# A slot table for the expert rows, an even split of the first expert weights, and filler products on TensorE

## The chip, the cores and the metric

The kernel runs as one program on one core of a Trainium2 chip. Its time is the device time of one execution in microseconds (us). Everything is float32, except one product in bfloat16.

## What is computed

The reference is a small vision transformer with four layers over 16 images of 37 tokens (592 tokens) with 192 features. The arithmetic of the earlier sublayers is not touched by the change. The last sublayer is a mixture of eight experts, of which each token takes the two with the highest gates:

```python
logits = xf @ Wr + br                       # xf: 592 x 192, eight experts
gates = jax.nn.softmax(logits, axis=-1)
top_g, top_i = jax.lax.top_k(gates, 2)
out = jnp.zeros_like(xf)
for e in range(8):
    w_e = jnp.sum(top_g * (top_i == e), axis=-1)
    h = jax.nn.gelu(xf @ W1[e] + b1[e], approximate=False)   # W1[e]: 192 x 768
    y = h @ W2[e] + b2[e]                                     # W2[e]: 768 x 192
    out = out + w_e[:, None] * y
```

`xf` is the layer-normalised `h`, and the result is added to `h`.

## The kernel before

**Tower.** The 16 images are held as eight pairs; a pair fills 101 partitions (37 tokens, a gap up to 64, 37 tokens). Each layer is cut into phases (`T` transposes the normalised rows, `F` and `K` make keys and queries, `R` turns them, `S` scores, `W` values, `X` turns the probabilities, `O` the output of attention, `Z` turns it, `P` projects), and every phase is done for two halves of four pairs, q = 0 and q = 1. The string `ORDER` interleaves the phases of the two halves into `SCHEDULE`, and each of the five engines walks that list in its own stream, so an engine that waits holds back all that stands behind it in the list. A PSUM bank is a job: `start_job` on TensorE waits until the bank's last user has been read, `end_job` tells that it is filled. `A` to `G` are the sublayers before the last, `H` is the last one.

**Routing (`H`).** Phase `H,G` makes the gate logits of a half: for each pair three products whose contraction has 128, 64 and 1 rows. `route_gate` on VectorE marks the two picked experts (`picked`). Phase `H,C` (job `cum`) sums on TensorE how many tokens before this one picked the same expert, on top of the first row of that expert's region. `route_spots` on VectorE turns it into two row numbers for each token. GpSimd then scatters: for each of the 16 (pair, choice) it sends 101 rows of 194 numbers (the features, the gate and the token's own row number) to the DRAM tensor `expert_rows`, line L552, which had been filled with blank rows. While these run, TensorE counts the tokens of each expert and makes the bias part (`eb`), VectorE adds it to `h` and runs `plan_tiles`, which tells which expert the spare tiles belong to.

**Expert loop.** Each expert has one tile of 128 rows, and there are nine spare tiles, 17 in all. When all scatters have landed, SyncE loads the tiles from `expert_rows` (`load_x`, L407). For each tile TensorE turns the rows (`turn_x`, L1261 and L1262, into 128 and 64 feature rows), makes 12 products with W1 (`fc1`, L1274: six column blocks, for each one product over 128 rows and one over 64) and 6 products with W2 (`fc2`, L1285); ScalarE does the gelu (L730), VectorE copies the turned rows and weighs the result by the gate (`weigh_y`, L1175, three buffers `yb`), and GpSimd adds the 128 rows to `rows_out` in DRAM with an indirect DMA (L560). Each of these waits until the one before has landed (`added`), since two tiles may hold the same token. The order on TensorE is turn(j+1), fc1(j), fc2(j-1). There are three sets of weights. SyncE loads the next ones in one stream: W1 of tile j+3 when fc1(j) is done, then the rows of tile j+6 when add j has landed, then W2 of tile j+3 when fc2(j) is done. Last, SyncE copies `rows_out` to the output.

In the profile's names `arena_k` holds the tiles' rows, the weighed results and the third set of weights, `rep` the hidden rows after the gelu, `bank` a PSUM bank. A float32 product shows as two matmul records, a transpose as one.

## Time and profile before

| | |
|---|---|
| median of 3 runs (lowest, highest) | 630.85 us (627.7, 631.73) |
| the profiled execution's own time | 634.18 us |
| its span, first to last instruction | 632.4 us |
| TensorE busy | 512.4 us (81%) |
| VectorE, ScalarE, GpSimd busy | 269.5, 183.7, 120.2 us |
| mean granted TensorE clock | 0.829 of full speed |
| DMA | 39.29 MB, mean 62 GB/s |

### The profile page before, as it was taken

Reading aid. Unit: us, or ns where it says so; the run is one execution under the profiler, and the core shown is the slowest. Engines: PE = TensorE matmul, PEld = TensorE weight load, DVE = VectorE, ACT = ScalarE, POOL = GpSimd, SP = SyncE. Lnnn points to the kernel's source line nnn. Section 1 sums busy time; section 2 is a strip of 40 time slices with the busy share of each in tenths; the row PEclk is TensorE's granted clock in tenths of the full one; section 3 lists DMA queues with packets and bytes.
Section 4 is the critical chain, followed back from the end, with each engine's and each line's share of the span. In section 5 each row is a group of like instructions: output and inputs, shape, how many; then the busy total and the mean of one; then the engine's idle time right before and its main releaser. Section 6 shows DMA issues by size and latency. Waiting matters only on the chain.

```text
span 632.4 us, 8623 instructions
## 1 busy us (share of the span) xinstructions
PE 512.4 (81%) x3314; PEld 414.0 (65%) x3314; DVE 269.5 (43%) x735; ACT 183.7 (29%) x439; POOL 120.2 (19%) x127
## 2 busy tenths in 40 slices
PE   4899999796967798999999579755503999999992
PEld 4876766695846676877578458754402788777872
DVE  5467545435474745635355666853400011111100
ACT  0222323212323616346452255221100222222120
POOL 2220100011120110111001230117861021221121
PEclk9979569878886969999999879855555599999897
DMA  8800000000290000000050000200113137666742
GB/s 320 205 2 0 1 1 1 2 1 1 66 250 11 0 1 2 2 0 1 1 150 1 1 2 2 76 1 13 24 17 78 37 96 200 168 202 187 219 106 41
DMA packets 23725, 39.29 MB, mean 62 GB/s; under 512 B 6167, under 2 KB 16399, under 8 KB 23474
## 3 DMA queue, kind: packets, MB, share of 16 engines
q1 hardware_dynamic: 16484, 35.40, 19.3%
q0 software_dynamic: 7056, 2.69, 3.4%
q8 instruction: 27, 0.44, 0.3%
q10 hardware_dynamic: 144, 0.64, 0.3%
q14 instruction: 14, 0.11, 0.1%
HBM read 31.51 MB, written 7.91 MB: 62 GB/s over the span
## 4 chain that ended last, share of the span: by engine, by line
PE 64%; DVE 15%; POOL 6%; issue 5%; ACT 5%; DMA 3%; POOLq 0%; SPq 0%; DVEq 0%; ACTq 0%
PE bank L1274 14%; PE bank L1285 6%; PE bank L1231 5%; PE bank L1503 5%; PE bank L1251 5%; PE bank L1209 4%; POOL expert_rows L552 4%; PE bank L1411 4%; PE bank L1455 3%; PE bank L1298 3%; PE bank L1240 3%; PE bank L1470 2%; ACT xn L581 2%; DVE stats L758 2%; PE bank L1352 2%
## 5 line engine op out<-in xcount | busy, mean ns | idle before, releaser
L480 POOL TENSOR_TENSOR rstd<-rstd_tmp,minus_half 101x4 f32<-101x4 f32 x20 | 20.5, 1025 | 333.1 <-DVE rstd_tmp L768 333.1
L1274 PE MATMUL bank<-arena_k,weights 128*128 128x128 f32 (+1 forms) x288 | 68.5, 355 | 0.4 <-issue 0.2
L1274 PEld LDWEIGHTS bank<-arena_k,weights 128*128 128x128 f32 (+1 forms) x288 | 48.4, 210 | 19.9 <-issue 6.5
L1251 PE MATMUL bank<-weights,rep 96*111 96x192 f32 (+1 forms) x320 | 56.8, 327 | 0.0
L1175 DVE TENSOR_SCALAR arena_k<-bank,arena_k 128x192 f32<-128x192 f32 x17 | 7.1, 417 | 113.5 <-PE bank L1285 113.5
L1251 PEld LDWEIGHTS bank<-weights,rep 96*111 96x111 f32 (+1 forms) x320 | 52.2, 175 | 2.2 <-issue 2.1
L560 POOL DMA_INDIRECT rows_out<-arena_k x17 | 26.4, 1551 | 122.6 <-DVE arena_k L1175 112.9
L1231 PE MATMUL bank<-nT,weights 96*96 96x296 f32 (+1 forms) x144 | 42.9, 446 | 3.8 <-DVE nT L783 2.5
L730 ACT ACTIVATE rep<-bank,parameters 128x128 f32<-128x128 f32 x48 | 14.2, 366 | 87.2 <-PE bank L1274 87.2
L552 POOL DMA_INDIRECT expert_rows<-x_rows,spot_row x16 | 35.6, 2223 | 11.5 <-issue 10.6
L1503 PE MATMUL bank<-weights,oT 96*101 96x192 f32 (+1 forms) x144 | 34.9, 412 | 3.0 <-issue 1.8
L581 ACT ACTIVATE xn<-h,minus_mean_rstd,rstd 101x192 f32<-101x192 f32 x56 | 25.9, 535 | 37.5 <-POOL minus_mean_rstd L487 37.4
L1442 PE MATMUL bank<-vblk,et 111*37 111x51 f32 (+1 forms) x640 | 25.1, 243 | 13.9 <-ACT et L692 7.1
L1231 PEld LDWEIGHTS bank<-nT,weights 96*96 96x96 f32 (+1 forms) x144 | 24.9, 178 | 17.5 <-issue 7.5
L1209 PE MATMUL bank<-constants,x_y 101*96 101x101 f32 x144 | 21.6, 321 | 17.6 <-DVE x_y L1070 10.3
L1442 PEld LDWEIGHTS bank<-vblk,et 111*37 111x37 f32 (+1 forms) x640 | 24.0, 143 | 17.1 <-issue 16.2
L1503 PEld LDWEIGHTS bank<-weights,oT 96*101 96x101 f32 (+1 forms) x144 | 30.7, 220 | 6.6 <-ACT oT L645 4.4
L1411 PE MATMUL bank<-arena_k,qT 96*64 96x222 f32 (+1 forms) x320 | 34.3, 368 | 0.8 <-DVE arena_k L796 0.8
L805 DVE TENSOR_TENSOR vblk<-bank,constants 111x384 f32<-111x384 f32 x40 | 21.6, 554 | 23.8 <-PE bank L1251 15.7
L1261 PE MATMUL bank<-constants,arena_k 128*128 128x128 f32 x17 | 5.3, 313 | 32.5 <-DMA arena_k<-expert_rows 32.5
L1209 PEld LDWEIGHTS bank<-constants,x_y 101*96 101x96 f32 x144 | 18.8, 167 | 19.6 <-issue 12.9
L730 ACT ACTIVATE rep<-bank,expert_b 128x128 f32<-128x128 f32 x54 | 15.9, 365 | 51.1 <-PE bank L1274 51.1
(243 smaller groups left out, 891.9 us busy)
## 6 DMA issues: line engine op xcount, KB each, us to landing
weights<-in_w SPq DMA_DIRECT2D x12, 576.0 KB, 4.4
weights<-in_w SPq DMA_DIRECT2D x12, 384.0 KB, 4.5
expert_rows<-blank_row SPq DMA_DIRECT2D x1, 3977.0 KB, 22.3
arena_k<-in_w SPq DMA_DIRECT2D x5, 576.0 KB, 4.2
arena_k<-in_patches SPq DMA_DIRECT2D x4, 606.0 KB, 8.4
weights<-in_w SPq DMA_DIRECT2D x12, 192.0 KB, 5.3
arena_k<-in_w SPq DMA_DIRECT2D x5, 384.0 KB, 4.4
arena_k<-expert_rows SPq DMA_DIRECT2D x17, 97.0 KB, 2.1
```

The source lines that it names most:

```text
L552: g.indirect_dma_start(slots, bass.IndirectOffsetOnAxis(spot_row[0:ROWS, r, k:k + 1], 0), xa[0:ROWS, r, k, :], None, bounds_check=XROWS - ...
L560: g.indirect_dma_start(rows_out, bass.IndirectOffsetOnAxis(xt[j % XBUFS].bitcast(I32)[:, XW - 1:XW], 0), yb[j % 3], None, bounds_check=T + ...
L581: ins = sc.activation(dst, src, ACT.Identity, scale=rstd[0:ROWS, r:r + 1], bias=nmr[0:ROWS, r:r + 1])
L730: sc.activation(hT[b][:, m], PS[2 * b + half][:, TILE * x:TILE * x + TILE], ACT.Gelu, bias=bias[:, m:m + 1]).then_inc(gelu_done, 1)
L1209: last = nc.tensor.transpose(ps[0:96, 128 * p:128 * p + ROWS], src[0:ROWS, p, 96 * s:96 * s + 96], ident[0:ROWS, 0:ROWS])
L1231: last = mm(o, w(seg, k, col + 96 * s, 96), nt(k, q), start=(k == 0), stop=(k == 1 and not lora))
L1251: last = mm(o, nrep[q][k][0:96 + k, im], w(n + "_qkv", k, 2 * D, D), start=(k == 0), stop=(k == 1 and n != "B"))
L1274: last = mm(PS[2 * (j % 2) + half][:, TILE * x:TILE * x + TILE], w1b[j % WSETS][0:r, k, 128 * m:128 * m + 128], xT[j % 2][0:r, k], start=( ...
L1285: last = mm(PS[4 + j % 2][:, 0:D], hT[j % 2][:, m], w2b[j % WSETS][:, m], start=(m == 0), stop=(m == MT - 1))
L1411: last = mm(ps[GAP * i:GAP * i + m, HH * TOK * s:HH * TOK * s + HH * TOK], qT[s][:, TOK * im:TOK * im + m], kblk[q][s][:, im % Q8].rearran ...
L1442: last = mm(ps[GAP * pr:GAP * pr + m, VW * i + gw * g:VW * i + gw * (g + 1)], et[q][:, g, TOK * (im - Q8 * q):TOK * (im - Q8 * q) + m], vb ...
L1503: last = mm(ps[0:ROWS, D * i:D * i + D], pair_cols(oT, k, 2 * c + i), wp, start=(k == 0), stop=(k == 1))
```

## The change

**Slot table.** The scatters, the blank fill of `expert_rows` and the copy of the rows on GpSimd are gone. ScalarE writes the normalised rows of `H` to `xn` as in other layers, and SyncE stores them to `rows_x` in DRAM (8 direct DMAs) as soon as they are there. For each token and choice, VectorE compares the spot with the 42 first spots of the 41 columns (eight experts by five tiles deep, and one empty), which gives the column and the place in it (`hit`, 101 x 1024 a half); GpSimd multiplies the column mark with the token number and with the gate (`entry`, three operations a half); and TensorE sums 16 products of `hit` and `entry` into a table of 128 places by 41 columns, with token, gate and an occupied mark (job `table`). `slot_tables` turns it into `slot_row` and `slot_gate`. A tile's rows are then gathered by GpSimd with one indirect DMA (`gather`), six ahead of the loop and one behind each add from then on. For the nine spare tiles GpSimd reads the column from `tile_of` and copies two columns each. `plan_tiles` now runs ahead of the `eb` additions on VectorE.

**Weights.** The first expert weights and the turned rows are split into 96 and 96 rows, not 128 and 64. W1 is loaded by three DMAs, not two. VectorE copies the turned rows in one operation, not two. SyncE's stream in the loop has no wait on `added` any more.

**Fillers.** `keep_busy` runs n products of the 128 x 128 identity with itself into the bank that the next job will use, ahead of that job's waits. There are 198 of them by a fixed table.

```diff
+IDLE_T = {("B", 1): 11, ("D", 1): 8, ("F", 1): 25, ("G", 1): 9, ("H", 0): 10, ("H", 1): 12}
+IDLE_R = 19
+IDLE_O = {("B", 0): 12, ("C", 0): 12, ("C", 1): 15, ("G", 1): 14}
+IDLE_CUM, IDLE_SLOT, IDLE_ROWS = 9, 6, 8
...
             def load_w1(e, b):
-                sp.dma_start(w1b[b][:, 0], w1[e][:, 0]).then_inc(w1_loaded[b], 16)
-                sp.dma_start(w1b[b][0:D - 128, 1], w1[e][0:D - 128, 1]).then_inc(w1_loaded[b], 16)
+                sp.dma_start(w1b[b][:, 0], w1[e][0:HALF, 0]).then_inc(w1_loaded[b], 16)
+                sp.dma_start(w1b[b][0:128 - HALF, 1], w1[e][HALF:128, 0]).then_inc(w1_loaded[b], 16)
+                sp.dma_start(w1b[b][128 - HALF:HALF, 1], w1[e][0:D - 128, 1]).then_inc(w1_loaded[b], 16)
...
-            sp.wait_ge(scattered, 16 * TOPK * PAIRS)
-            for j in range(XBUFS):
-                load_x(slice(j * REGION, j * REGION + TILE), j)
+            for q in octs:
+                sp.wait_ge(*xn_ready.at(("H", q)))
+                store_rows(rows_x, xn, q, x_stored)
...
-                    sp.wait_ge(added, 16 * j + 16)
-                    load_x(slice(row, row + TILE) if n < NE else bass.ds(row, TILE), n % XBUFS)
...
                 if (n, ph) == ("H", "C"):
+                    pool.wait_ge(*begins_ready.at(q))
+                    link(g.tensor_tensor(col[:, :, 2], past_begin[0:ROWS, :, 0:COLS], past_begin[0:ROWS, :, 1:], ALU.subtract))
+                    link(g.tensor_tensor(col[:, :, 0].rearrange("p (c k) x -> p c k x", k=TOPK), col[:, :, 2].rearrange("p (c k) x -> p c k x", k=TOPK), which, ALU.mult))
                     pool.wait_ge(*spots_ready.at(q))
-                    for r in range(P8 * q, P8 * q + P8):
-                        for k in range(TOPK):
-                            g.indirect_dma_start(slots, bass.IndirectOffsetOnAxis(spot_row[0:ROWS, r, k:k + 1], 0), xa[0:ROWS, r, k, :], None,
-                                                 bounds_check=XROWS - 1, oob_is_err=False).then_inc(scattered, 16)
+                    g.tensor_tensor(col[:, :, 1], col[:, :, 2], gate, ALU.mult).then_inc(*entries_ready.inc(q))
...
+            def gather(j):
+                at = slot_row[:, DEEP * j:DEEP * j + 1] if j < NE else tile_row[:, j - NE:j - NE + 1]
+                g.indirect_dma_start(xt[j % XBUFS], None, rows_x, bass.IndirectOffsetOnAxis(at, 0),
+                                     bounds_check=T + TILE - 1).then_inc(x_loaded[j % XBUFS], 16)
+            pool.wait_ge(slots_ready, 1)
+            pool.wait_ge(x_stored, 16 * 4 * len(octs))
+            for j in range(XBUFS):
+                gather(j)
+            pool.wait_ge(plan_ready, 2)
+            for j in range(SPARE):
+                col = pool.value_load(tile_of[0:1, 1, j:j + 1], min_val=0, max_val=COLS - 1)
+                g.tensor_copy(tile_row[:, j:j + 1], slot_row[:, bass.ds(col, 1)]).then_inc(spares_ready, 1)
+                g.tensor_copy(tile_gate[:, j:j + 1], slot_gate[:, bass.ds(col, 1)]).then_inc(spares_ready, 1)
             for j in range(TILES):
                 pool.wait_ge(y_ready, j + 1)
                 if j:
                     pool.wait_ge(added, 16 * j)
...
+                if j + XBUFS < TILES:
+                    pool.wait_ge(xT_filled, j + 1)
+                    gather(j + XBUFS)
...
+            slot_tables()
+            plan_tiles()
             for c in range(PAIRS // 2):
                 add_bank(("eb", c), h[0:ROWS, 2 * c:2 * c + 2], h[0:ROWS, 2 * c:2 * c + 2])
-            plan_tiles()
...
+            def keep_busy(j, n):
+                b, k = where[j]
+                if k:
+                    pe.wait_ge(bank_read[b], k)
+                for _ in range(n):
+                    mm(PS[b][:, 0:128], ident, ident, start=True, stop=True)
...
-                        for k, r in enumerate((128, D - 128)):
-                            last = mm(PS[2 * (j % 2) + half][:, TILE * x:TILE * x + TILE], w1b[j % WSETS][0:r, k, 128 * m:128 * m + 128], xT[j % 2][0:r, k],
+                        for k in range(2):
+                            last = mm(PS[2 * (j % 2) + half][:, TILE * x:TILE * x + TILE], w1b[j % WSETS][:, k, 128 * m:128 * m + 128], xT[j % 2][:, k],
                                       start=(k == 0), stop=(k == 1))
```

On TensorE, from the gate logits of the second half to the first products of the expert loop, the instructions stood like this before (`picked,every` is the running sum, `disp` the turned gates, `expert_b` the bias part):

```order
574 L1352 MATMUL bank<-parameters,ones 101x8
575 L1359 MATMUL bank<-picked,before 101x32
576 L1362 MATMUL bank<-picked,every 101x32 x4
...
580 L1363 MATMUL bank<-region_base,ones 101x32
581 L1508 MATMUL bank<-picked,every 1x8 x8
582 L1514 MATMUL bank<-constants,disp 8x101 x8
583 L1522 MATMUL bank<-expert_b,x_y 101x192 x8
584 L1261 MATMUL bank<-constants,arena_k 128x128
585 L1262 MATMUL bank<-constants,arena_k 64x128
```

and now, with the fillers as L1272 and L1613 and the table as L1445:

```order
587 L1424 MATMUL bank<-parameters,ones 101x8
588 L1272 MATMUL bank<-constants 128x128 x9
589 L1432 MATMUL bank<-picked,before 101x32
590 L1435 MATMUL bank<-picked,every 101x32 x4
...
594 L1436 MATMUL bank<-region_base,ones 101x32
595 L1272 MATMUL bank<-constants 128x128 x6
596 L1445 MATMUL bank<-vblk,arena_e 128x123 x16
597 L1594 MATMUL bank<-picked,every 1x8 x8
598 L1600 MATMUL bank<-constants,disp 8x101 x8
599 L1608 MATMUL bank<-expert_b,x_y 101x192 x8
600 L1613 MATMUL bank<-constants 128x128 x8
601 L1331 MATMUL bank<-constants,arena_k 96x128 x4
```

Fillers came in at three places, the table's 16 products between the running sum and the count, and the turned rows have 96 partitions both times.

On GpSimd, from the second half's routing to the end, before:

```order
94 L552 DMA expert_rows<-x_rows,spot_row 5248x194 x8
95 L545 COPY x_rows<-x_rows 101x4x192
96 L552 DMA expert_rows<-x_rows,spot_row 5248x194 x8
97 L560 DMA rows_out<-arena_k 720x192 x17
```

and now (the rows of the eight further spare tiles are left out):

```order
99 L568 TENSOR_TENSOR vblk<-vblk,share 101x8x41 [waits spots_ready,pool_chain]
100 L573 DMA arena_k<-rows_x,slot_row 128x192 [waits blanked,x_stored,slots_ready,entries_ready]
101 L573 DMA arena_k<-rows_x,slot_row 128x192 x5
102 L584 TENSOR_LOAD tile_of [waits plan_ready]
...
105 L585 COPY tile_row<-slot_row 128x1
106 L586 REGISTER_ALU
107 L586 COPY tile_gate<-slot_gate 128x1
...
156 L594 DMA rows_out<-arena_k,slot_row 720x192 [waits y_ready,rows_stored,spares_ready]
157 L573 DMA arena_k<-rows_x,slot_row 128x192 [waits xT_filled]
158 L594 DMA rows_out<-arena_k,slot_row 720x192 [waits added,y_ready]
159 L573 DMA arena_k<-rows_x,slot_row 128x192 [waits xT_filled]
```

The 16 scatters are gone, six gathers and 18 small copies stand ahead of the first add, and a gather stands between every two adds up to the eleventh.

## Rows read from the trace of the kernel before

**Rows 1.** The page, part 2: granted TensorE clock in 40 slices of the span

```profile
PEclk9979569878886969999999879855555599999897
```

**Rows 2.** The chain of waits from 433 us: start, length, what

```profile
433.64 4.86 PE bank L1352 x23
...
475.21 7.21 DMA expert_rows<-x_rows,spot_row
482.44 2.01 DMA arena_k<-expert_rows
...
485.81 8.75 PE bank L1274 x24
...
515.56 4.80 PE bank L1274 x24
520.36 2.15 PE bank L1285 x12
```

**Rows 3.** Busy time by stretches: PE, PEld, DVE, ACT, POOL, clock, DMA share, GB/s

```profile
61.50:88.80 27.30, 25.16 (x106) 19.93 (x103) 14.20 (x44) 6.84 (x15) 1.71 (x3) 0.50 0.00 1
...
406.20:484.60 78.40, 29.95 (x197) 26.73 (x197) 26.63 (x109) 9.74 (x22) 40.87 (x24) 0.50 0.10 16
484.60:508.60 24.00, 23.87 (x71) 17.45 (x71) 2.25 (x9) 3.54 (x12) 0.00 (x0) 0.50 0.24 59
508.60:580.30 71.70, 71.70 (x378) 56.64 (x378) 7.42 (x29) 18.27 (x65) 15.56 (x10) 1.00 0.62 175
```

**Rows 4.** The same, sum of five stretches at the lower clock between 122.9 and 372.1 us

```profile
sum 61.50, PE 44.90 PEld 38.59 DVE 26.95 ACT 17.43 POOL 7.73; mean PE 8.98 PEld 7.72 DVE 5.39 ACT 3.49 POOL 1.55
```

**Rows 5.** TensorE in order of time: last bracket the idle time before and its end

```profile
76.81 1.58 PE L1209 MATMUL bank<-constants,xn 101*96 101x101 f32 x8 [0.58 <-ACT xn L581]
121.93 2.81 PE L1442 MATMUL bank<-vblk,et 111*64 111x51 f32 x64 [2.96 <-ACT et L692]
155.60 4.25 PE L1209 MATMUL bank<-constants,x_y 101*96 101x101 f32 x24 [5.01 <-DVE x_y L1070]
271.62 6.24 PE L1455 MATMUL bank<-nT,weights 96*128 96x296 f32 x24
362.39 1.58 PE L1209 MATMUL bank<-constants,xn 101*96 101x101 f32 x8 [6.32 <-ACT xn L581]
431.43 0.94 PE L1217 MATMUL bank<-constants,x_rows 101*128 101x101 f32 x4 [6.04 <-ACT x_rows L581]
```

**Rows 6.** GpSimd's groups of instructions: count, busy us, mean ns, idle before

```profile
L552 POOL DMA_INDIRECT expert_rows<-x_rows,spot_row x16 | 35.6, 2223 | 11.5 <-issue 10.6 <-POOL x_rows L545 0.9
L500 POOL TENSOR_TENSOR h<-h,parameters 101x768 f32<-101x768 f32 x4 | 7.5, 1866 | 8.3 <-ACT xn L581 8.2
```

**Rows 7.** The adds (L560) to landing: from 508 to 540 us, then 544 to 600

```profile
DMA to landing us min/median/max: 3.5/3.6/4.0
...
DMA to landing us min/median/max: 5.2/6.0/7.7
```

**Rows 8.** GpSimd in order of time: the fifth last add and the last

```profile
600.61 1.54 POOL L560 DMA_INDIRECT rows_out<-arena_k  x1 [6.95 <-DMA rows_out<-arena_k]
...
624.86 1.54 POOL L560 DMA_INDIRECT rows_out<-arena_k  x1 [2.74 <-DMA rows_out<-arena_k]
```

**Rows 9.** VectorE in order of time, second half's routing, last bias addition, plan

```profile
438.92 0.19 DVE L886 TENSOR_REDUCE gate_rows<-bank 101x4 f32<-101x32 f32 x1 [5.38 <-PE bank L1352]
439.37 0.42 DVE L891 TENSOR_TENSOR et<-gates 101x256 f32<-101x256 f32 x1
441.20 0.19 DVE L897 SCALAR_TENSOR_TENSOR picked<-gates,valid 101x32 f32<-101x32 f32 x1
...
452.15 0.56 DVE L850 TENSOR_TENSOR h<-bank,h 101x384 f32<-101x384 f32 x1 [0.72 <-PE bank L1522]
452.63 0.14 DVE L940 COPY plan<-bank 1x8 f32<-1x8 f32 x1
...
455.50 0.15 DVE L955 TENSOR_SCALAR tile_of<-plan 1x9 int32<-1x9 f32 x1
```

More of the change, by code:

```diff
@@ L121, in phase_jobs @@
     if (n, ph) == ("H", "C"):
-        return [("cum", q)]
+        return [("cum", q)] + [("table",)] * q
     if ph == "G":
@@ L921, in route_spots @@
[L921 to L925 removed]
+                mark(v.tensor_reduce(high, at, AX.X, ALU.max))
+                link(v.tensor_reduce(both, at, AX.X, ALU.add))
@@ new lines, in route_spots, with slot_tables @@
+                link(v.scalar_tensor_tensor(depth[0:ROWS], depth[0:ROWS], -float(TILE), spots, ALU.mult, ALU.add))
+                v.tensor_tensor(hit[0:ROWS, n * q:n * q + n], depth[0:ROWS].unsqueeze(2).broadcast_to([ROWS, n, TILE]),
+                                lane[0:ROWS].unsqueeze(1).broadcast_to([ROWS, n, TILE]), ALU.is_equal).then_inc(*hits_ready.inc(q))
+                dve.wait_ge(*hits_ready.at(q))
+            def slot_tables():
+                j = ("table",)
+                dve.wait_ge(*filled(j))
+                row, gate, busy = (bank(j)[:, COLS * x:COLS * x + COLS] for x in range(3))
+                link(v.tensor_scalar(unused[:], busy, 1.0, spare_row[:], ALU.subtract, ALU.mult))
+                v.tensor_tensor(slot_row[:], row, unused[:], ALU.add).then_inc(slots_ready, 1)
+                v.tensor_copy(slot_gate[:], gate).then_inc(*freed(j))
+                dve.wait_ge(*evacuated(j))
@@ L1363, in _ @@
                     end_job(("cum", q), mm(ps[0:ROWS, 0:w8_], ones[:, 0:ROWS], base[:], start=False, stop=True))
+                    if q:
+                        keep_busy(("table",), IDLE_SLOT)
+                        ps = start_job(("table",))
+                        n_ = PAIRS * TOPK
+                        for x in range(n_):
+                            if x % (n_ // 2) == 0:
+                                pe.wait_ge(*hits_ready.at(x // (n_ // 2)))
+                                pe.wait_ge(*entries_ready.at(x // (n_ // 2)))
+                            last = mm(ps[:, 0:3 * COLS], hit[0:ROWS, x], entry[0:ROWS, x].rearrange("p w c -> p (w c)"), start=(x == 0), stop=(x == n_ - 1))
+                        end_job(("table",), last)
                 elif ph == "G":
@@ L1525, in _ @@
             wait_evacuated(*[max((j for j in order if where[j][0] == b), key=lambda j: where[j][1]) for b in range(8)])
+            for _ in range(IDLE_ROWS):
+                mm(PS[6][:, 0:128], ident, ident, start=True, stop=True)
             turn_x(0)
```

169 lines of the change are left out of this document (99 added, 70 removed).

## The prediction

> **What bounds the kernel now.** I read the clock row of the page first, then the chain of waits, then stretches. The clock row shows that TensorE is granted full speed in the middle but half of it in patches on the left and for a long piece on the right [rows 1]. The chain shows two things about the last quarter. From 438 to 484.6 us it lies not on TensorE but on the scatters: 16 of them at 2.2 us with 0.3 us between, 7.21 us until the last has landed, 2.01 us for loading the first tile [rows 2, 6]. TensorE is busy 30 of 78 us there [rows 3]. Then the expert loop is TensorE alone: from 508.6 to 580.3 us it is busy without a break [rows 3], and one tile costs 4.80 (fc1) + 2.15 (fc2) + 0.22 (two transposes) = 7.17 us [rows 2]. Its first fc1 took 8.75 us, since the clock stood at 0.50 until 508.6 us [rows 2, 3]. So the last part has two limits in a row, GpSimd's scatters and TensorE's products; the part before 406 us is TensorE with short waits for VectorE and ScalarE, after which the clock falls [rows 5].
>
> **Part 1, the even split.** Before, 24 matmul records of 128 moving columns take 4.80 us, 0.200 us each, and the six products of fc2, though with 192 columns, only 2.15/12 = 0.179 us each [rows 2]. Fewer columns should not take longer. The nearest record with 96 rows on both sides and 128 stationary columns is L1455: 24 records of 296 columns in 6.24 us, 0.260 each [rows 5], by columns 0.112 us for 128. I take it, since it has the same rows, the same stationary width and the same clock: fc1 = 24 x 0.112 = 2.7 us. The ends: 2.7 us, and 4.80 us if rows don't matter. What stands out is that fc1 changes between 128 and 64 rows after every product, and L1455 does not. The Trainium skill ("TensorEngine Tiling (Array Packing)", Key Properties) says that a change of the tiling mode drains the engine, and that contractions of up to 64 rows are tiled; by it the split pays, as the row of L1455 has it. Another page of the Trainium skill ("TensorE: Matmul & The Clock Gate", LDWEIGHTS) says that loading weights takes a time by columns and not by rows; by that alone fc1 stays as it is (second rival). A tile on TensorE then costs 2.7 + 2.1 + 0.2 = 5.0 us. ScalarE (six gelus) and VectorE are at 18 and 7 of 72 us in the loop [rows 3] and stay hidden. The third W1 DMA costs nothing as long as weights are ahead.
>
> **Part 2, routing.** Counted on the clock of before, from the transposes of the second half at 431.4 us [rows 5]. If the fillers hold the full clock: transposes 0.9 (four records take 0.94 cold [rows 5], eight as much at full clock), an estimate of 0.6 for the copies, gate logits 3.0 (4.86 cold [rows 2]; half is 2.4), the pick on VectorE 2.4 as before [rows 9], the running sum's 22 records at some 0.1 each 2.1, together 440.4. New on VectorE: seven small operations of 0.1 to 0.2 us, two of 336 elements at 0.5, and the hit marks of 1024 elements: 256 take 0.42 [rows 9], so at most 1.7. Sum 4.3, 444.7. GpSimd's three operations of 328 elements run beside it: 768 take 1.87 [rows 6], so 0.8 each, hidden. The table: the first half's eight products are done while VectorE works, the second half's are 16 records, 1.8 us; VectorE makes the columns in 0.5: 447.0. From here two branches. The gather: issue 0.8, landing 3.6 (an add of 128 rows when DMA is quiet [rows 7]), 451.4. No gather is in the trace; the ends are 2.0 (a direct load of a tile [rows 2]) and 7.2 (a scatter [rows 2]), which is 449.8 and 455.0. I take the add because it has the same queue and 128 rows. The other branch is VectorE's: the plan now comes first, 3.0 us (452.63 to 455.65), then four bias additions of 0.56 [rows 9], and only after them TensorE may run its last 8 fillers, 1.8 us: 454.1. So what sets the start of the loop is this branch, and I take 454.5 against 484.6 before: 30 us earlier. The late filler is in that sum; without it 1.8 us less.
>
> **Part 3, GpSimd in the loop.** This is where I expect the next limit. An add waits until the last one has landed. One began at 600.61 less 6.95 idle less 1.55, at 592.1; with 7.7 us to landing that is 599.8, and the next began at 600.6 [rows 7, 8]. So the period of adds is landing + 0.8. The gather between (about 1.6 us of GpSimd) hides inside the flight. The landing is 3.5 to 4.0 us early in the loop and 5.2 to 7.7, median 6.0, from 544 to 600 us [rows 7], when SyncE's weight loads run right beside the adds. That gives 4.4 to 6.8 us a tile, against TensorE's 5.0. Before, 7.17 hid either. The same 1.2 MB of weights now come every 5 to 6 us, staggered by fc1 and fc2, so that some load is nearly always in flight, but rarely both: I take 5.8 (the middle, 5.6, leaning to the loaded rows) for 13 tiles and 5.0 for the last three, whose loads are over; 16 periods make 90.4 us. The first add: two transposes and copy 0.8, two fc1 5.4, one fc2 2.1, weighing and issue 1.2, that is 9.5 after the start: 464.0. The six gathers (six times 1.9 from 447.8) and the 18 small copies are done by about 461, so they cost nothing; if the copies took over 0.35 us each more than I think, they would delay it. From the start of the last add to the end of the span it was 632.4 - 624.86 = 7.5 us [rows 8]. End: 464.0 + 90.4 + 7.5 = 561.9 us.
>
> **Part 4, the fillers ahead of the last sublayer.** A filler product is two records of 128 columns, 0.22 us at full and 0.45 at half clock. Where it stands in a wait that is long enough it is free: 12 take 2.7 in a wait of 2.96, 19 take 4.3 in 5.01, 25 take 5.6 in 6.32 [rows 5]; the other sites up to 407 us, four more with waits of 2.9 to 5.3, are alike. After five of these stretches TensorE worked 44.9 us at half clock [rows 4]; at full clock it would be 22.4. Much of that is behind other engines too, VectorE being busy 27.0 of 61.5 us [rows 4], so I count 60%: 13.5. The last O, gate logits and transposes before the second half's give 3.5 more. The site of half 1 in B has no wait to speak of, 0.58 us [rows 5], and 11 products cost 4.9 us cold, in a stretch of 25.2 busy us at half clock [rows 3]; if they bring the full clock forward by some us, it evens out, and I set it at nothing, with -4 to +4. Sum: 17 us, from 8 (a third of the cold work) to 25 (all of it).
>
> **Sum.** Span 561.9 - 17 = 544.9 us; with the 1.8 us around it 546.7, against 634.2 of the profiled execution. That one lay 3.3 above the median, so the forecast for the median is 543.4 us. Low end: GpSimd never late, 16 x 5.0, and 25 from the fillers: 464.0 + 80 + 7.5 - 25 - 1.5 = 525. High end: 13 x 6.8 + 15, and 8 from the fillers: 464.0 + 103.4 + 7.5 - 8 - 1.5 = 565.4.
>
> **Rivals.** *TensorE stays the bound.* Adds land in 4.2 us or less throughout, as they did until 540 us [rows 7]; the period is 5.0: 464.0 + 80 + 7.5 - 17 - 1.5 = 533 us. For it: weights no longer come in one burst with the add. Against: more bytes a microsecond. Chance 0.22.
>
> *The split brings nothing.* fc1 stays at 4.80, as it would if a product's time went by columns alone (the weight rule above). Against it speaks L1455. Period 7.2, first add at 468.2: 468.2 + 115.2 + 7.5 - 17 - 1.5 = 572.4 us. Chance 0.10.
>
> *The fillers don't hold the clock.* Then they run at 0.45 us and overrun seven of the waits by 2 to 5 us each, 23 in all, with 4 for the site in B and 2 in the last sublayer, nothing is given back, and routing runs cold, 8 us more: 561.9 + 29 + 8 - 1.5 = 597.4 us. For it: 24 us of unbroken work from 484.6 did not lift the clock [rows 3]. Against: those were fc1's products with their change of rows, and 128-row products leave no holes. Chance 0.09.
>
> *Slower than before.* Gathers and adds share GpSimd's queue. If an add could not run beside a gather, and a gather landed as late as a scatter did (median about 6.8, last 7.2 [rows 2]), each of the first 11 periods would be 6.0 + 6.8 + two issues of 0.8 = 14.4, the other five 6.8: 464.0 + 192.4 + 7.5 - 17 - 1.5 = 645 us. It decides from 13.1 us a period on. Nothing in the trace shows such a series; scatters there started every 2.5 us while the earlier ones were in flight. Chance 0.02.
>
> **Chances.** My forecast 0.56, the rivals as given, 0.01 for the rest. The range 524 to 573 takes in the bounds, the first and the second rival, and leaves out about 0.12. About 1% is what three runs with this spread (627.7 to 631.7) can tell from no change. Faster by over 1%: 0.97; within 1%: 0.01; slower: 0.02.
>
> **What the profile after would show.** Part 1: fc1 at 2.6 to 2.8 us a tile. Part 2: the loop starting at about 437.5 (454.5 - 17), 47 us earlier in all, with the last bias addition and the fillers just ahead of it. Part 3: GpSimd's adds idle before on "DMA rows_out", not on VectorE, starts 5 to 6.5 us apart, and TensorE with holes of up to 1.5 us a tile. Part 4: clock digits of 9 to the left of the loop. The forecast is wrong if the landing under load is not near 5, if GpSimd's dynamic copies are slow enough to delay the first add past 464, or if holes in the loop bring the clock down again.

## The result, and the profile after

The changed kernel takes **568.09 us** (median of four runs, 562.93 to 570.62) against 629.28 for the kernel before beside it (four runs, 625.57 to 631.73): ratio 0.902, 95% interval 0.894 to 0.910. From here on medians are of all runs of a kernel, while ratios with their intervals leave out its slower runs, so that the two need not agree. The forecast was 543.4 us with a range of 524 to 573: faster as said, inside the range, 25 us above the number. The profiled execution took 562.93 us with a span of 561.2; it is the fastest of its four, 5.2 below their median.

The marks below stand for both profiled executions, in us from the start of the span. "First transposes" are those of the gate's second half; "first turn" is the first transpose of gathered rows, where the expert loop begins.

| | before | after | forecast for after |
|---|---|---|---|
| first transposes | 431.4 | 419.6 | 414.4 (431.4 - 17) |
| first turn | 484.6 | 449.65 | 437.5 |
| first add | 509.0 | 460.1 | 447.0 |
| last add | 624.9 | 553.4 | 537.4 |
| end of the span | 632.4 | 561.2 | 544.9 |
| fc1 of one tile at full clock, from its start to that of fc2 | 4.80 | 2.68 | 2.7 |
| mean period of the adds | 7.24 | 5.83 | 5.65 |

The page, part 2, in the 40 slices of the span (compare [rows 1]):

```profile
POOL 3040100002111010102200012310220544434332
PEclk9999777989989899999999999799976899998895
```

The patches of half clock on the left have become 7s and 8s, and the long cold piece before the loop is down to a 7 and a 6 (slices 30 and 31); the middle is as it was. The stretches that answer to [rows 3], with the same columns: the last sublayer and the routing, the first tile, and two parts of the loop:

```profile
398.20:449.60 51.40, 41.12 (x294) 38.65 (x291) 30.78 (x111) 8.96 (x19) 14.34 (x18) 0.78 0.11 28
449.60:461.20 11.60, 11.52 (x92) 11.02 (x91) 2.01 (x5) 4.42 (x15) 3.52 (x20) 0.94 0.36 100
461.20:508.60 47.40, 45.30 (x345) 44.72 (x344) 6.79 (x18) 16.40 (x58) 20.09 (x16) 0.97 0.98 273
```

The DMA share in the loop is 0.98 where it was 0.62, since the same weights now come in less time. TensorE is no longer busy without a break there. TensorE in order of time from the first transposes into the loop (compare [rows 2, 5]; L1272 and L1613 are fillers):

```profile
419.63 0.96 PE L1286 MATMUL bank<-constants,xn 101*128 101x101 f32 x8 [2.47 <-ACT xn L616]
421.80 0.91 PE L1424 MATMUL bank<-parameters,nT 128*101 128x8 f32 x4 [1.21 <-issue]
...
426.98 3.99 PE L1272 MATMUL bank<-constants 128*128 128x128 f32 x18
...
433.97 1.95 PE L1445 MATMUL bank<-vblk,arena_e 101*128 101x123 f32 x16
438.06 2.05 PE L1445 MATMUL bank<-vblk,arena_e 101*128 101x123 f32 x16 [2.14 <-DVE arena_e L969]
...
441.66 2.91 PE L1608 MATMUL bank<-expert_b,x_y 8*101 8x192 f32 x16 [0.29 <-issue]
446.10 3.76 PE L1613 MATMUL bank<-constants 128*128 128x128 f32 x16 [1.53 <-DVE h L885]
449.65 1.06 PE L1331 MATMUL bank<-constants,arena_k 128*96 128x128 f32 x4
...
453.92 2.84 PE L1344 MATMUL bank<-arena_k,weights 96*128 96x128 f32 x24
456.60 2.12 PE L1355 MATMUL bank<-weights,rep 128*128 128x192 f32 x12
```

With two halves of 96 rows fc1 is 24 records in 2.84 us here, and fc2 starts 2.68 us after it: in order of time the last record counts to its end, which overlaps the next one. The like figures of before are 4.97 and the 4.80 of [rows 2]; its TensorE in order of time has

```profile
536.90 4.97 PE L1274 MATMUL bank<-arena_k,weights 128*128 128x128 f32 x24
```

The fillers are 0.118 us a record where the clock is up (experiment 12 below, 42 in 4.96 us), and 0.22 to 0.235 in the two groups here: both stand where the clock is down, and the second is what TensorE does right before the loop. VectorE in the same place (compare [rows 9]):

```profile
436.78 1.22 DVE L969 TENSOR_TENSOR arena_e<-depth,lane 101x1024 f32<-101x1024 f32 x1
...
440.60 0.20 DVE L979 TENSOR_TENSOR slot_row<-bank,unused 128x41 int32<-128x41 f32 x1
...
440.95 0.15 DVE L996 COPY plan<-bank 1x8 f32<-1x8 f32 x1
...
443.86 1.93 DVE L885 TENSOR_TENSOR h<-bank,h 101x384 f32<-101x384 f32 x4
```

The hit marks, the table's rows, then the plan (2.9 us), then the four bias additions, then the fillers: the order that the forecast walked through, later by what the next section takes apart. GpSimd in order of time, gathers (L573), one of the small copies, adds (L594), and then the adds' time to landing before and after 540 us (compare [rows 6 to 8]):

```profile
441.79 1.34 POOL L573 DMA_INDIRECT arena_k<-rows_x,slot_row  x1 [5.07 <-DVE slot_row L979]
...
452.50 0.18 POOL L586 COPY tile_gate<-slot_gate 128x1 f32 x1
460.12 1.64 POOL L594 DMA_INDIRECT rows_out<-arena_k,slot_row  x1 [7.43 <-DVE arena_k L1236]
...
489.40 1.58 POOL L594 DMA_INDIRECT rows_out<-arena_k,slot_row  x1 [4.35 <-DMA rows_out<-arena_k,slot_row]
491.29 1.06 POOL L573 DMA_INDIRECT arena_k<-rows_x,tile_row  x1 [0.32 <-issue]
496.84 1.58 POOL L594 DMA_INDIRECT rows_out<-arena_k,slot_row  x1 [4.49 <-DMA rows_out<-arena_k,slot_row]
```

```profile
DMA to landing us min/median/max: 3.6/5.5/6.6
...
DMA to landing us min/median/max: 3.4/3.5/3.5
```

The copies are over 7.4 us before the first add. From then on an add waits for the landing of the last one, 7.4 us from one to the next here, and only after it may the gather go. The waits between 461 and 540 us:

```profile
POOL rows_out L594 <- DMA rows_out<-arena_k,slot_row: 23.2, 7, 4.5
...
POOL rows_out L594 <- DMA rows_out<-arena_k,tile_row: 11.9, 3, 5.8
...
PE bank L1331 <- DMA arena_k<-rows_x,tile_row: 5.7, 3, 2.1
```

Ten adds waited 35.1 us for the one before. TensorE waited three times, 5.7 us, and not for the adds but for gathers that stand behind them in the queue. From these waits alone either could be what sets the loop's pace. The chain of waits that ends the span says more; its shares from 460 to 554 us:

```profile
by line: DMA rows_out<-arena_k,slot_row 46.0%; DMA rows_out<-arena_k,tile_row 38.8%; issue 12.9%; POOLq L182 1.9%; POOLq L594 0.5%; DVE arena_k L1236 0.5%; POOLq L573 0.3%; POOLq L592 0.3%; DVEq L1232 0.0%
```

84.8% of it is adds in flight, and TensorE's last product ended at 542.8 us, 10.6 us before the last add began. Experiment 7 tests it.

### The profile page after: what moved, and what is told of

Its sections match the earlier page's. It is cut to its first block, busy times and chain, and to the rows that moved or that the text cites. A ratio compares the mean times of both kernels' runs of the same rounds, so it can differ in the third digit from the quotient of the medians.

```text
span 561.2 us, 9551 instructions
## 1 busy us (share of the span) xinstructions
PE 490.3 (87%) x3742; PEld 421.8 (75%) x3742; DVE 274.5 (49%) x725; ACT 183.6 (33%) x439; POOL 108.3 (19%) x150
## 4 chain that ended last, share of the span: by engine, by line
PE 50%; DVE 19%; DMA 15%; issue 6%; ACT 6%; POOL 2%; POOLq 1%; SPq 0%; DVEq 0%; ACTq 0%
DMA rows_out<-arena_k,slot_row 8%; PE bank L1320 7%; DMA rows_out<-arena_k,tile_row 6%; PE bank L1300 6%; PE bank L1589 5%; PE bank L1495 5%; PE bank L1368 3%; PE bank L1541 3%; PE bank L1278 3%; PE bank L1309 3%; PE bank L1556 3%; ACT xn L616 3%; DVE stats L793 2%; PE bank L1424 2%; DVE arena_e L848 1%
## 5 line engine op out<-in xcount | busy, mean ns | idle before, releaser
L497 POOL TENSOR_TENSOR rstd<-rstd_tmp,minus_half 101x4 f32<-101x4 f32 x20 | 20.5, 1024 | 321.1 <-DVE rstd_tmp L803 321.1
L1272 PE MATMUL bank<-constants 128*128 128x128 f32 x380 | 49.3, 290 | 0.0
L1272 PEld LDWEIGHTS bank<-constants 128*128 128x128 f32 x380 | 47.5, 205 | 1.0 <-issue 0.2
L1344 PE MATMUL bank<-arena_k,weights 96*128 96x128 f32 x288 | 35.6, 282 | 0.1
L1344 PEld LDWEIGHTS bank<-arena_k,weights 96*128 96x128 f32 x288 | 34.4, 198 | 0.5 <-DVE arena_k L1226 0.5
L1495 PEld LDWEIGHTS bank<-arena_k,qT 96*64 96x64 f32 (+1 forms) x320 | 24.1, 135 | 12.5 <-issue 4.1
L1368 PE MATMUL bank<-tok_w,arena_k 128*101 128x192 f32 x96 | 18.8, 366 | 8.1 <-DMA arena_k<-in_patches 8.1
L654 ACT ACTIVATE arena_k<-bank,constants 96x296 f32<-96x296 f32 x48 | 19.9, 505 | 18.1 <-PE bank L1300 9.5
L1355 PE MATMUL bank<-weights,rep 128*128 128x192 f32 x144 | 25.8, 330 | 0.0
L1368 PEld LDWEIGHTS bank<-tok_w,arena_k 128*101 128x101 f32 x96 | 18.0, 193 | 8.6 <-issue 8.1
L1355 PEld LDWEIGHTS bank<-weights,rep 128*128 128x128 f32 x144 | 23.9, 195 | 0.0
```

Source lines behind the costliest of these rows:

```text
L497: link(g.tensor_tensor(rstd[0:ROWS, a], rtmp[0:ROWS, a], mhalf[0:ROWS, a], ALU.pow))
L654: ins = sc.activation(kblk[q][0][:, :, x], src, ACT.Copy, scale=mask[:, x:x + 1])
L1272: mm(PS[b][:, 0:128], ident, ident, start=True, stop=True)
L1344: last = mm(PS[2 * (j % 2) + half][:, TILE * x:TILE * x + TILE], w1b[j % WSETS][:, k, 128 * m:128 * m + 128], xT[j % 2][:, k], start=(k == ...
L1355: last = mm(PS[4 + j % 2][:, 0:D], hT[j % 2][:, m], w2b[j % WSETS][:, m], start=(m == 0), stop=(m == MT - 1))
L1368: last = mm(ps[0:ROWS, D * i:D * i + D], patch[q][:, 2 * c - P8 * q + i, k], tokw[:, k], start=(k == 0), stop=(k == PATCH_K - 1))
```

## The experiments

Theory A, with which I went in: the split gives what the 96-row record said; the loop is then paced by the series of adds at landing + 0.8 us, with TensorE next at 4.85 us a tile; the fillers give some 17 us. The rivals: the fillers give little, or they are what matters and the rest is small; in the loop, TensorE or the gathers set the pace. Medians are of kernels timed beside the kernel before (633.4 to 633.9 us in those groups). The marks of each profiled execution, in us:

| kernel | median | first transposes | first turn | first add | last add |
|---|---|---|---|---|---|
| split alone | 609.7 | 422.3 | 475.7 | 488.6 | 596.4 |
| no split | 595.9 | 426.2 | 456.3 | 471.5 | 582.9 |
| no fillers | 575.0 | 422.0 | 453.1 | 465.3 | 557.7 |
| before with fillers | 625.2 | 420.9 | 474.6 | 498.6 | 618.1 |
| changed kernel again | 567.2 | 426.4 | 456.4 | 466.9 | 553.3 |
| no routing fillers | 558.4 | 426.3 | 456.0 | 468.2 | 560.8 |
| two targets | 551.3 | 419.4 | 449.4 | 459.9 | 534.2 |
| no weight reloads | 550.8 | 420.2 | 454.3 | 464.6 | 541.3 |
| two targets, no routing fillers | 556.6 | 425.6 | 455.4 | 467.6 | 541.9 |
| two targets, no fillers | 562.9 | 426.6 | 457.7 | 469.9 | 545.1 |
| no turn fillers | 565.1 | 421.8 | 452.3 | 465.9 | 556.3 |
| two targets, longer filler | 554.7 | 420.3 | 451.5 | 461.8 | 536.1 |

**1. The split alone**, in the kernel before:

```diff
-w1b = [x[:, 0:2 * HID]...
+w1b = [x[0:HALF, 0:2 * HID]...
-nc.tensor.transpose(PS[6 + j % 2][:, 0:TILE], xt[j % XBUFS][:, 0:128], ident)
-nc.tensor.transpose(PS[6 + j % 2][0:D - 128, TILE:2 * TILE], xt[j % XBUFS][:, 128:D], ident)
+for k in range(2):
+    nc.tensor.transpose(PS[6 + j % 2][0:HALF, TILE * k:TILE * k + TILE], xt[j % XBUFS][:, HALF * k:HALF * k + HALF], ident)
```

> The kernel before with the 96 and 96 split alone (scatters and no fillers, SyncE's stream still waits for each add). Theory A (a tile costs TensorE 5.0 us, and the serial adds, landing + 0.8, are the limit of the loop): fc1 at 2.7 to 2.9 us, adds 5.8 to 6.5 us apart, the loop some 20 to 30 us shorter, 600 to 610 us. Theory B (the split pays only because rows are gathered by then, since the loads of the rows behind each add hold the loop here): under 10 us gained, 620 us or more.

609.7 us (605.8 to 618.3), ratio 0.971 with an interval of 0.936 to 1.006, wide because the runs scatter. The interval takes in 1, and the profile is plainer than the time. TensorE in order of time, then what GpSimd's adds waited for and their landing:

```profile
507.67 2.84 PE L1277 MATMUL bank<-arena_k 96*128 96x128 f32 x24
```

```profile
  DMA rows_out<-arena_k: 61.5, 12
...
DMA to landing us min/median/max: 3.5/6.3/8.7
```

fc1 falls by 2.1 us from this edit alone, 4.97 to 2.84 in order of time or 0.207 to 0.118 us a record, and 12 of 17 adds turn to waiting for the one before. The period is 6.74 us: slightly above what A gave.

What in the 128 and 64 rows costs the time, the trace of the changed kernel tells in two other places, both at a granted clock of 1.00. First 12 records of 64 rows that follow each other, with 296 columns; then 32 records of 192 columns whose row counts change between 96 and 97 after every product (the line shows the first form):

```profile
286.57 3.26 PE L1541 MATMUL bank<-nT,weights 64*128 64x296 f32 x12
330.37 5.39 PE L1320 MATMUL bank<-weights,rep 96*111 96x192 f32 x32
```

The first is 0.27 us a record, against 0.26 for the same columns with 96 rows (L1455 in [rows 5]), so few rows alone cost next to nothing. Nor do 128 rows alone cost anything, as the fillers show. The second is 0.168 us a record for 192 columns, 0.112 for 128, so not every change of the row count costs either. What is left is the change between 128 and 64 rows. A tile has 12 of them, the last one ahead of fc2, and by TensorE's 7.17 us a tile before and 4.85 after each costs 0.19 us, an estimate.

**2. The changed kernel without the split** (the same diff the other way round):

> The changed kernel with the old 128 and 64 split. Theory A: TensorE is the limit again at 7.2 us a tile and the adds wait for it, the loop 18 to 25 us longer than in the changed kernel, 587 to 595 us, fc1 at 4.8 us. Theory B (adds and gathers limit the loop so far that the split hardly matters): within 8 us of the changed kernel, 568 to 576 us.

595.9 us (587.0 to 603.7). TensorE, and what the adds waited for:

```profile
506.00 4.97 PE L1341 MATMUL bank<-arena_k,weights 128*128 128x128 f32 x24
```

```profile
  DVE arena_k L1234: 76.4, 15
```

fc1 is back at 5 us at full clock, the period at 6.96, and 15 of 17 adds wait for VectorE, that is for TensorE's products. The adds no longer pace the loop. In the finished kernel the split is worth 28 us by the medians and 24 by the fastest run of each, and all eight runs of the changed kernel, 562.9 to 570.6, lie below these four.

**3. The changed kernel without any filler:** every filler count set to 0.

> The changed kernel without the 198 filler products. Theory A (fillers hold the clock, and what they give is larger than what they delay): half clock after the waits before 406 us as before, the last sublayer's transposes 10 to 12 us later, in all 575 to 583 us. Theory B (fillers overrun about as much as they give back): within 4 us of the changed kernel.

575.0 us (567.1 to 578.6), 7 to 8 above the changed kernel by the medians; but the interval of its ratio, 0.898 to 0.937, takes in the changed kernel's 0.902, so this run alone does not show a gain. Its clock row is at half speed in many more places (the changed kernel's is above):

```profile
PEclk9989958969799896999999998699555579999875
```

and yet its first transposes stand at 422.0 us, not at the 431.4 of before.

**4. The kernel before with the fillers** of the tower and of the cumulative counts:

```diff
+                    if (n, q) in IDLE_T:
+                        keep_busy(("nT", n, q, 0), IDLE_T[n, q])
                     pe.wait_ge(*xn_ready.at((n, q)))
```

> The kernel before with the fillers of the tower and the running sum alone (not those before the table and before the loop, which belongs to the new routing). Theory A: the last sublayer's transposes 11 to 12 us earlier as in the changed kernel, and all of it kept, 615 to 620 us. Theory B: less than 5 us, since the fillers at half clock overrun, 625 us or more.

625.2 us (ten runs, 619.7 to 630.2), ratio 0.991, interval 0.984 to 0.998: 9 us by the medians but 6 by the ratio, with an interval of 1 to 10. That is a third to a half of the 17 us that I had costed, and the time meets B's bound (625 or more), not A's 615 to 620, while the gain is over B's 5 us.

**5. The changed kernel once more**, unchanged:

> The changed kernel as it is, for a second measurement beside the next three. Theory A (its time is set by where its clock falls and varies by itself): the median lies at 563 to 571 us, as in its first four runs (562.9 to 570.6), and the first turn of rows and the first add lie within 6 us of 449.7 and 460.1. Theory B (the first profile is typical as it stands): the same rows within 1 us.

567.2 us, as before. But the profile shows how much one profile can be taken for: the same program had its first transposes at 426.4, 6.8 us later than in its first profile, while the loop from first to last add took 86.4 us in place of 93.3. The clock row:

```profile
PEclk9987768898989979999999999989977979989995
```

The falls of the clock lie elsewhere in it. Theory A's bound of 6 us for the first turn and the first add was too narrow by a little (6.8 both).

**6. Without the fillers of the routing stretch:** `IDLE_CUM, IDLE_SLOT, IDLE_ROWS = 0, 0, 0`.

> The changed kernel without the fillers of the routing stretch alone (none ahead of the cumulative counts, the slot table and the first turn of rows; the fillers of the tower stay). Theory A: in the changed kernel's trace the last 8 fillers ran at the low clock for 3.76 us right ahead of the first turn of rows, with nothing behind them to wait for, and the 9 ahead of the counts took 3.99 us. Without them the first turn comes 3 to 6 us earlier (444 to 447), the first add at 454 to 457, and the time falls by 2 to 5 us. Theory B (they keep the clock up for the first tiles): the first turn comes earlier but the first tiles run at the low clock, fc1 above 4 us in tiles 0 and 1, the first add is within 1 us of 460 and the time within 1.5 us.

558.4 us, but from 552.4 to 570.3: the interval of the ratio, 0.853 to 0.908, takes in the changed kernel's 0.904, and the profiled execution is the slowest of the four. Two of the four, 552.4 and 553.1, lie below all eight runs of the changed kernel (562.9 to 570.6). What can be read in it is the stretch. From first transposes to first turn it took 29.7 us, as with the fillers (30.0), and then the first fc1 was cold:

```profile
449.69 5.41 PE L1608 MATMUL bank<-expert_b,x_y 8*101 8x192 f32 x16
...
457.15 4.83 PE L1344 MATMUL bank<-arena_k,weights 96*128 96x128 f32 x24
```

so that the first add came 42.0 us after the first transposes, against 40.5 with the fillers, in both profiles of the changed kernel. The bias products are cold too, 5.41 us in place of the 2.91 shown above, and so are the table's, 3.77 us twice in place of 1.95 and 2.05: cold work takes back what the fillers took, and the stretch is no shorter without them. It is theory B's mechanism (cold work in place of the fillers), and it outweighs what is saved by 1.5 us.

**7. Two targets for the adds:**

```diff
+dest, added = [rows_out, rows_odd], [sem("added_even"), sem("added_odd")]
...
-    pool.wait_ge(added, 16 * j)
+    pool.wait_ge(added[j % 2], 16 * (j // 2))
...
+g.dma_start(rows_out[0:T]..., rows_odd[0:T]..., accum_op=ALU.add).then_inc(folded, 16)
```

> The changed kernel with the adds of even and odd tiles going to two DRAM tensors (the second zeroed long before), so that add j waits for add j-2 alone; one accumulating DMA adds the second tensor to the first after the last add. Theory A (the series of adds sets the loop, TensorE is next at 4.85 us a tile): the adds' period falls from 5.83 to 4.9 to 5.2 us, 16 periods give 10 to 15 us back, the fold costs 4 to 7 us at the end, and the time falls by 4 to 10 us, to 558 to 564. Theory B (the landings are long because the queues are full, and two adds in flight stretch each other): landings rise to 8 us or more, the period stays at 5.5 or above, and the time rises by the fold, to 570 to 575.

**551.3 us** (548.9 to 551.9), ratio 0.878, interval 0.867 to 0.890: better than A had it. The stretch of the loop that stands above at 45.30 busy of 47.40, and GpSimd in order of time:

```profile
460.00:508.00 48.00, 48.00 (x378) 47.64 (x377) 7.44 (x20) 18.27 (x65) 26.36 (x20) 1.00 1.00 281
```

```profile
503.39 1.58 POOL L602 DMA_INDIRECT rows_odd<-arena_k,tile_row  x1 [1.91 <-DVE arena_k L1247]
505.27 1.07 POOL L579 DMA_INDIRECT arena_k<-rows_x,tile_row  x1 [0.30 <-DMA rows_out<-arena_k,tile_row]
508.24 1.58 POOL L602 DMA_INDIRECT rows_out<-arena_k,tile_row  x1 [1.91 <-DVE arena_k L1247]
...
534.18 1.54 POOL L602 DMA_INDIRECT rows_out<-arena_k,tile_row  x1 [0.41 <-issue]
537.93 0.92 POOL L609 DMA_DIRECT2D rows_out<-rows_odd  x1 [2.21 <-DMA rows_out<-arena_k,tile_row]
```

TensorE has no hole, 15 of GpSimd's 17 adds wait for VectorE and only one, at the end, for a landing, and the adds come every 4.85 us (4.64 on average, since the last two follow each other at 1.95), although the DMA share is 1.00. The profile gives no landing times for these adds, so whether landings grew longer, as theory B has it, is not shown; the period did not. The late gathers are gone as well, though nothing was done to them: they were late because they stood behind adds that waited. The last add comes 74.3 us after the first (changed kernel 93.3); the tail from it grows from 7.8 to 13.0 us by the fold. 19.0 - 5.2 = 13.8 us, and the spans differ by 561.2 - 547.2 = 14.0. That the adds pace the changed kernel's loop is hereby shown. The Trainium skill ("DMA: Bandwidth & Descriptors", Rules for kernel authors) says that nothing guards the bytes of an accumulating DMA between its read and its write, so that another one to the same bytes must wait for its semaphore; the second tensor takes away the need for that wait, not the wait alone.

**8. No weight reloads in the loop:**

```diff
-                load_w1(e, nxt % WSETS)
                 sp.wait_ge(fc2_done, j + 1)
-                load_w2(e, nxt % WSETS)
```

TensorE's waits for the weights now ask for the first load of each set alone.

> The changed kernel with the expert weights loaded for tiles 0 to 2 only: the loop leaves out the reload of weights for tiles 3 to 16, which multiply by the weights of the first three experts. Theory A (the reloads are what stretches the landing of an add from 3.5 to 4.2 to 6.6 us): all landings are 3.4 to 3.8, the period of adds falls to TensorE's 4.85 to 5.0, and the last add comes 12 to 15 us earlier (loop from first turn to last add 89 to 92 in place of 103.7). Theory B (gathers and the add's own descriptors set the landing): landings stay at 4.5 to 6 in the middle of the loop and the period at 5.4 or more.

550.8 us in its one run, so the time says little and the profile is what counts. The adds over the whole loop:

```profile
DMA to landing us min/median/max: 3.4/3.5/4.9
```

Two landings of 17 are above 3.6 (4.5 and 4.9), the period is 4.79, and the last add comes 76.7 us after the first. It is the weights' reloads that stretch a landing from 3.5 to 5.5 us. From first turn to last add it is 87.0 us, below A's 89 to 92.

**9. Two targets and no routing fillers** (edits 6 and 7 together):

> The candidate for the best version: two targets for the adds, and no fillers in the routing stretch (none ahead of the cumulative counts, the slot table and the first turn of rows). Theory A (the two savings stand in different stretches, so they add up: 568.1 to 551.3 from the targets, and 567.2 to 558.4 from the late fillers, the latter between runs that scatter by 18): 541 to 549 us, 543 taken. Theory B (what the late fillers took was scatter of the clock's falls, worth nothing by itself): 549 to 553.

556.6 us (550.3 to 557.4), ratio 0.891, interval 0.881 to 0.900: neither theory. From first transposes to first add it is 42.0 us, as in 6, against 40.5 in 7. Here their removal costs 5.3 us by the medians (the runs, 550.3 to 557.4 against 548.9 to 551.9, touch, and so do the intervals of the ratios). Nothing here bears out the two low runs of experiment 6, and I take them for scatter; what the routing fillers are worth in the changed kernel itself stays open.

**10. Two targets and no fillers:** all counts 0.

> Two targets for the adds and no fillers at all, the tower's left out too. Theory A (the tower's fillers give some 5 to 9 us, as before's 625.2 against 633.9 with them, and the routing stretch's cost 4): 2 to 6 us above the kernel with two targets and no late fillers, 546 to 553. Theory B (fillers only move the falls of the clock about): within 1.5 us of it.

562.9 us (559.7 to 564.1), ratio 0.903, interval 0.896 to 0.909: 6.3 above 9 and 11.6 above 7. That is A's upper end against 9, and the interval is clear of 7's (0.867 to 0.890). A's time of 546 to 553 was missed, since 9 itself came out slower than thought.

**11. Without the 8 fillers ahead of the first turn alone:** `IDLE_ROWS = 0`.

> The changed kernel without the 8 fillers ahead of the first turn of rows, all others kept. Theory A (in its trace they run at the low clock for 3.76 us while the rows had landed 4 us before): the first turn 2 to 4 us earlier, the time 564 to 567 against 567.2 to 568.1. Theory B (the loop is held by its series of adds from the first add on, and the first tiles run at the low clock without them): first add within 1 us of 460 when the clock's falls lie as in the first profile, the time within 1 us of 567 to 568.

565.1 us (558.3 to 566.6), ratio 0.903, interval 0.892 to 0.915: 2 to 3 us below the changed kernel by the medians, and not to be told from it. In the profile the stretch from first transposes to first add is 44.1 us against 40.5, and the first turn came after 30.5 us against 30.0, not 2 to 4 us earlier. The first two tiles' fc1:

```profile
453.45 5.49 PE L1344 MATMUL bank<-arena_k,weights 96*128 96x128 f32 x24
...
459.16 3.39 PE L1344 MATMUL bank<-arena_k,weights 96*128 96x128 f32 x24
```

They are 3.06 and 2.84 us in the changed kernel's trace. So theory B's mechanism, cold first tiles, is in this profile, though neither theory's numbers are confirmed and the medians give no verdict.

**12. A longer filler before the gate's second half**, with two targets: `("H", 1): 12` becomes `("H", 1): 21`, which fills the wait of 2.5 us after which the clock fell.

> The kernel with two targets for the adds and all fillers, with 21 in place of 12 fillers ahead of the transposes of the gate's second half: they fill the 2.49 us in which TensorE waited there (from 416.91 to 419.40 us), after which the clock fell at 420.10 and stayed low for 10.24 us. Theory A (that gap let the clock fall, and the fall cost the gate's products and the nine fillers behind them about half of their 9.2 us): the clock stays at its upper level from 413 to at least 437 us, the time from the first of these transposes to the first turn of rows falls from 30.0 to 24 to 27 us, and the median from 551.3 to 546 to 549. Theory B (the falls follow from what ran long before, and move with it): the clock falls somewhere within 10 us of there all the same, the stretch stays at 29.5 us or more, and the median within 2 us of 551.

554.7 us (550.9 to 560.1), ratio 0.886, interval 0.878 to 0.894; nothing gained: 3.3 above 7 by the medians, with intervals that overlap. TensorE in order of time:

```profile
414.96 4.96 PE L1283 MATMUL bank<-constants 128*128 128x128 f32 x42
420.27 0.91 PE L1297 MATMUL bank<-constants,xn 101*128 101x101 f32 x8 [0.35 <-ACT xn L627]
...
426.29 4.21 PE L1283 MATMUL bank<-constants 128*128 128x128 f32 x18
...
438.12 3.65 PE L1456 MATMUL bank<-vblk,arena_e 101*128 101x123 f32 x16 [2.15 <-DVE arena_e L980]
```

The wait is closed, the first half of the gate's products is at full clock, and then the clock falls all the same, at 424.6 us while the gate's small products run, so that the 9 fillers behind are cold again (0.234 us a record), and once more at 438.3, where the table's second half takes 3.65 us in place of 2.05. The stretch to the first turn is 31.2 us. Theory B's mechanism (its bound of 2 us for the median was missed by 1.3): the fall moved, it did not go.

## Why the prediction was right, and where it was 25 us low

The changed kernel's span was 16.3 us longer than forecast: 5.2 ahead of the first transposes, 6.9 in the routing, 1.0 from first turn to first add, 2.9 in the adds, 0.3 in the tail. The other 8.5 us are no stretch of the kernel: I took 3.3 off for the profiled execution of before lying above its median, and the one of after lay 5.2 below its own.

**Part 1** was right: 2.68 us for fc1 against 2.7 by the same measure, from a record of another stage that had the same rows. Experiments 1 and 2 show the cause both ways; the rival, that fc1 goes by columns alone and stays as it was, is out. The rule of the Trainium skill on draining at a change of tiling mode ("TensorEngine Tiling (Array Packing)", Key Properties) went the way that these runs show. That the cost sits in the change between 128 and 64 rows, and not in either row count, is shown by the two rows under experiment 1; that the engine drains there is that rule's word for it, and the trace shows only the time lost, some 0.19 us a change.

**Part 3** was right in mechanism and nearly in size: landing + 0.8, 5.83 against 5.65. The landing between 3.5 and 6.6 is the reloads' doing (8), the adds pace the loop (7), the gathers' lateness is a consequence. The second profile of the same kernel had 5.40, so the term scatters by about 7 us over the loop. The copies were far from mattering.

**Part 2** had the right order of steps and three sizes too small, two of them of the same sort: I counted TensorE's routing work and the last fillers on a held clock. The third is VectorE's. From first transposes to the end of the cumulative counts it took 13.0 us, not 9.0: transposes and copies 2.2 for 1.5, the gate's products 5.2 for 3.0, the cold fillers 3.8 where I had let VectorE's pick of 2.4 set the time and hide them, the counts 1.85 for 2.1. From there to the plan 8.35 for 6.6: VectorE's small operations took 5.4 for 4.3. And the 8 last fillers 3.5 for 1.8. Plan and bias additions were as forecast (5.15 for 5.3 together). From the split alone to the split with the new routing (1 against 3, no fillers in either) the medians differ by 34.7 us. In the profiles the first add is 23.3 us earlier, and the adds from first to last take 92.3 in place of 107.8. That second part, 15.5 us, I had not costed as a part of its own: it went in unnoticed with the landing I took. Whether it comes of the gathers in place of SyncE's row loads or of the wait that SyncE's stream lost, no run separates.

**Part 4** was mis-sized, the step being that 60% of the cold work comes back: 17 us forecast. By the medians the fillers give 7 to 8 us in the changed kernel (3, not clear of noise), 9 in the kernel before (4; 6 by the ratio), 12 with two targets (10 against 7, the one pair whose intervals are well apart). The profiled pair seems to show 11.8 us ahead of the first transposes; but without tower fillers these stood at 431.4, 422.3, 422.0 and 426.6, with them at 419.4 to 426.4 in ten profiles (means 425.6 and 422.7). The profile of before, on which the forecast rested, has the latest of the four without fillers; so most of the 11.8 us is the choice of the profile. What failed is the premise that work in place of a wait holds the clock: the long gaps to VectorE are filled, and the clock still falls, for some 3 to 10 us a time in the changed kernel's first profile and once for 17 us in its second (granted clock 0.50 from 62.4 to 79.0 us), and at places that move between executions (5, 12). The Trainium skill ("TensorE: Matmul & The Clock Gate", What's actually happening) says that the gate observes activity in a rhythm of its own, which a kernel's start does not reset. The two profiles of one program agree with it: their falls lie at other places, and the first transposes at 419.6 and 426.4 us. Whether more or wider filler products between the gate's own would hold it was not tried.

**The best version** is two targets with all fillers: 551.3 us, ratio 0.878 against 0.902 and 0.904. Its loop is TensorE alone at 4.85 us a tile. The fold, 5.2 us, and the routing's 30 us are next.

## What to carry to other kernels

Before costing a change by a profile, ask what the same program's second profile would say: here one stretch moved by 7 us and another by 7 the other way, at equal time. Where transfers that add to the same tensor run in series, their period is the landing time and the next issue (0.8 us here), and the landing time depends on what else is being loaded; a second target costs one fold at the end and frees the whole queue behind them. Fillers gave 6 to 12 us here, of 17 forecast: count on a part of the cold work, and count them at the cold price wherever the clock may be down. Where a contraction has to be split over rows, give neighbouring products the same row count: 96 and 96 cost 2.68 us a tile where 128 and 64 cost 4.80.

## What the runs showed of the hardware that I had not expected

- An f32 matmul record of 128 columns took 0.118 us with two halves of 96 rows or with fillers of 128 rows, and 0.207 us where 128 and 64 rows alternate (24 in 4.97 us); 64 rows in a row and a change between 96 and 97 rows cost nothing extra (experiment 1).
- An add of 128 rows landed in 3.5 us with no other load, a median of 5.5 and up to 6.6 beside the weights, and up to 8.7 in experiment 1; yet with two targets, at a DMA share of 1.00, an add could start every 4.85 us.
- A gather of 128 rows took 1.06 us of GpSimd where the scatter of 101 took 2.22 [rows 6], and a dynamic copy of one column 0.18.
- The clock fell in the middle of the gate's small products, with a wait of 1.27 us ahead of them and none among them (12).
